# Keys, values and queries of four tiles in one step, and attention one step closer to the convolution

## The reference, cut to what matters

```python
t = _to_tokens(x)
t = t + _L1_attn_ref(_ln_t(t), Wq, Wk, Wv)     # causal, one head of 128, softmax over the tokens before
t = t + _L1_ffn_ref(_ln_t(t), gate_w, gate_b, weight1, weight2)
```

## Time and profile before

| what | value |
|---|---|
| median of 3 runs | 2902.15 us (2899.94 to 2903.96) |
| the profiled execution | 2897.93 us, its span 2895.9 us |
| busy share PE, PEld, DVE, ACT, POOL | 93%, 73%, 65%, 62%, 61% |
| mean granted TensorE clock of the span | 0.977 |
| images 1 to 6, each | about 327.6 us |

### The profile page before, as it was taken

How to read it: one execution, slowest core, us unless ns; L and a number is a source line. 1 busy time by engine, 2 the same in 40 slices (tenths; PEclk the granted TensorE clock), 3 DMA queues, 4 the chain that set the end, 5 groups by cost and what they waited for, 6 DMA issues and landing times. The chain is left out here.

```text
span 2895.9 us, 53454 instructions
## 1 busy us (share of the span) xinstructions
PE 2702.8 (93%) x19102; PEld 2123.3 (73%) x19102; DVE 1887.0 (65%) x7235; ACT 1785.9 (62%) x4118; POOL 1758.3 (61%) x1831
## 2 busy tenths in 40 slices
PE   5688999999999999999999999999999998899787
PEld 3466787778777887778777787778777787777664
DVE  3466675767577775866677775866677766765425
ACT  3455666666675666666676666666676666665430
POOL 5777775776577755776577755776577756750000
PEclk8899999999999999999999999999999999999889
DMA  6455334633255324633255323643255323432199
GB/s 187 119 148 139 112 114 120 169 110 103 86 158 140 109 86 118 164 117 98 88 156 141 113 84 118 155 124 97 85 158 152 116 84 95 126 82 95 28 397 394
DMA packets 218212, 382.59 MB, mean 132 GB/s; under 512 B 43849, under 2 KB 128777, under 8 KB 217051
## 3 DMA queue, kind: packets, MB, share of 16 engines
q0 software_dynamic: 88992, 250.76, 30.0%
q1 hardware_dynamic: 126363, 113.95, 13.1%
q10 hardware_dynamic: 2592, 14.45, 1.2%
HBM read 316.90 MB, written 62.13 MB: 131 GB/s over the span
## 5 line engine op out<-in xcount | busy, mean ns | idle before, releaser
L532 POOL DMA_INDIRECT shared<-pair_table,idx x1800 | 1737.8, 965 | 836.4 <-issue 527.7
L1144 PEld LDWEIGHTS bank_o<-vals,prob_t 128*128 128x128 f32 x5200 | 634.4, 192 | 130.3 <-ACT prob_t L579 65.3
L1144 PE MATMUL bank_o<-vals,prob_t 128*128 128x128 f32 x5200 | 663.2, 277 | 31.5 <-ACT prob_t L579 31.5
L579 ACT ACTIVATE prob_t<-bank_r 128x512 f32<-128x512 f32 (+3 forms) x728 | 383.3, 548 | 479.8 <-PE bank_r L1131 479.0
L834 DVE CUSTOM_DVE_ANT_0 prob<-bank_r,mask 128x512 f32<-128x512 f32 (+3 forms) x728 | 449.9, 628 | 310.4 <-PE bank_r L1122 308.0
L1122 PE MATMUL bank_r<-keys,qt 128*128 128x512 f32 (+3 forms) x1456 | 640.7, 556 | 0.0
L824 DVE SCALAR_TENSOR_TENSOR shared<-shared,wb 128x128 f32<-128x128 f32 x1800 | 516.6, 347 | 160.4 <-ACT shared L560 159.7
L560 ACT ACTIVATE shared<-shared,wa 128x128 f32<-128x128 f32 x1800 | 561.6, 392 | 42.7 <-DMA shared<-pair_table,idx 42.6
L1111 PEld LDWEIGHTS bank_r<-convw_t,smp_t 128*128 128x128 f32 x3600 | 444.2, 194 | 56.8 <-issue 36.3
L1111 PE MATMUL bank_r<-convw_t,smp_t 128*128 128x128 f32 x3600 | 477.5, 279 | 1.5 <-ACT smp_t L565 1.5
L1131 PE MATMUL bank_r<-ident,prob 128*128 128x128 f32 x2600 | 382.2, 274 | 13.8 <-ACT prob L657 13.8
(11 more groups left out here) (168 smaller groups left out, 2235.7 us busy)
## 6 DMA issues: line engine op xcount, KB each, us to landing
shared<-in_dram SPq DMA_DIRECT2D x32, 1024.0 KB, 17.9
shared<-pair_table,idx POOLq DMA_INDIRECT x1800
pair_table<-rows_out SPq DMA_DIRECT2D x112, 256.0 KB
t<-in_dram SPq DMA_DIRECT2D x48, 256.0 KB, 3.9
t_dram<-t SPq DMA_DIRECT2D x48, 256.0 KB
shared<-in_dram SPq DMA_DIRECT2D x7, 1568.0 KB
stage<-t_dram POOLq DMA_DIRECT2D x8, 832.0 KB, 7.5
pm_dram<-logit SPq DMA_DIRECT2D x8, 800.0 KB
```

Of the source, the lines that this page charges most:

```text
L532: pool.indirect_dma_start(g[t % RING][:, n, :], None, pair_table[b % 2], bass.IndirectOffsetOnAxis(ap=idx[:, b % 2, i * TAPS + n:i * TAPS ...
L579: act.activation(prob_t[q % 3][:, 0:w], ring_bank(("prob", t, c))[:, 0:w], ACT.Copy)\
L1144: last = pe.matmul(attn_ps, prob_t[q % 3][:, n * P:(n + 1) * P], vals[:, slot(tb, at), :], start=(at == 0), stop=(at == ti))
```

## The change

It sets the three lags to 5, 6 and 7 and moves "keys", "vals" and "query" of each group into the one step 4n + 4: keys at F, vals at M, query at L. Before, keys were at L of that step and vals and query in the step after. All other units keep their places.

```diff
-LAG_S, LAG_V, LAG_T = 6, 7, 8
+LAG_S, LAG_V, LAG_T = 5, 6, 7
 MISC = (
-    (0, "E", "vals", -1, 5), (0, "M", "query", -1, 5), (0, "L", "keys", -1, 6),
-    (1, "E", "vals", -1, 6), (1, "M", "query", -1, 6),
+    (0, "F", "keys", -1, 6), (0, "M", "vals", -1, 6), (0, "L", "query", -1, 6),
     (2, "L", "turn_xf", -1, 4),
     (3, "E", "logit", -1, 4), (3, "F", "gstat", 1, 0),
-    (4, "L", "keys", 0, 0),
-    (5, "E", "vals", 0, 0), (5, "M", "chunk", 1, 0), (5, "L", "query", 0, 0),
+    (4, "F", "keys", 0, 0), (4, "M", "vals", 0, 0), (4, "L", "query", 0, 0),
+    (5, "M", "chunk", 1, 0),
     (6, "M", "chunk", 1, 1), (6, "L", "turn_xf", -1, 5),
     (7, "E", "logit", -1, 5), (7, "F", "turn", 1, 0), (7, "M", "chunk", 1, 2), (7, "L", "turn_xf", -1, 6),
-    (8, "E", "logit", -1, 6), (8, "M", "chunk", 1, 3), (8, "L", "keys", 0, 1),
-    (9, "E", "vals", 0, 1), (9, "F", "turn", 1, 1), (9, "M", "chunk", 1, 4), (9, "L", "query", 0, 1),
+    (8, "E", "logit", -1, 6), (8, "F", "keys", 0, 1), (8, "M", "chunk", 1, 3), (8, "M", "vals", 0, 1), (8, "L", "query", 0, 1),
+    (9, "F", "turn", 1, 1), (9, "M", "chunk", 1, 4),
     (10, "M", "chunk", 1, 5),
     (11, "F", "turn", 1, 2), (11, "M", "chunk", 1, 6),
-    (12, "F", "turn", 1, 3), (12, "M", "pm", -1, 0), (12, "L", "keys", 0, 2), (12, "L", "pm", -1, 1),
-    (13, "E", "vals", 0, 2), (13, "F", "pm", -1, 2), (13, "M", "query", 0, 2), (13, "L", "pm", -1, 3),
+    (12, "F", "turn", 1, 3), (12, "F", "keys", 0, 2), (12, "M", "pm", -1, 0), (12, "M", "vals", 0, 2), (12, "L", "pm", -1, 1), (12, "L", "query", 0, 2),
+    (13, "F", "pm", -1, 2), (13, "L", "pm", -1, 3),
     (14, "M", "pooled", -1, 0), (14, "L", "turn_xf", 0, 0), (14, "L", "turn_pooled", -1, 0),
     (15, "E", "logit", 0, 0), (15, "L", "turn_xf", 0, 1),
-    (16, "E", "logit", 0, 1), (16, "L", "keys", 0, 3),
-    (17, "E", "vals", 0, 3), (17, "M", "query", 0, 3),
+    (16, "E", "logit", 0, 1), (16, "F", "keys", 0, 3), (16, "M", "vals", 0, 3), (16, "L", "query", 0, 3),
...
```

## The result

| | before | after |
|---|---|---|
| median | 2902.3 us (2899.9 to 2904.0, 4 runs) | 3062.6 us (3059.3 to 3067.3, 4 runs) |
| ratio, 95% interval | | 1.056 (1.0546 to 1.0573) |
| span of the profiled execution | 2895.9 us | 3062.1 us |
| mean granted clock of the span | 0.977 | 0.965 |
| images 1 to 6, each | 325.9 to 327.6 us | 348.4 to 351.7 us |

The change makes the kernel 160 us slower; 3068 us was forecast. In kernel.py of after every line from the table on stands three lines higher: L1029 is L1032 of before, L1059 is L1062, L1100 is L1103.

The account below looks back on a forecast made before the run. PE's own queue was taken as the bound, except early in image 0, where POOL sets the pace. Terms 108 + 38.5 + 30 - 5 - 5 = 166.5 us on 2897.9 us gave 3064 us, stated as a 3068 us median; range 2985 to 3135 us.

Parts of the forecast that it names:

- Term 1: Keys steps of each image: at F, PE waits for DVE's normalising, 1.4 to 3.5 us each; 108 us in all.
- Term 2: Step 14, images 1 to 7: DVE's gate rows wait for "pooled" of the same step, PE loses 5.5 us; 38.5 us.
- Term 3: PE's clock: 2.5 more stretches per image at the lower level behind the new holes, 1.7 us each; 30 us.
- Terms 4 and 5: Pipeline drained one step earlier, -5 us; shifted waits for samples (steps 16, 17) and exponential (step 6 to 5), -5 us.
- Rival A: PE's existing idle time swallows the holes, later waits vanish, clock stays up: 78 us slower, 2980 us; 13%.
- Rival B: Each new hole on PE brings the lower clock: 95 us instead of 30, 3133 us; 8%.
- Rival C: Not slower: PE, 73% full by weight loads, has room for the stalls; only term 4's gain is left, 2893 us; 6%.

Follow-up runs that it names:

- the table without the lags: Kernel before with the new places of keys, vals and query but old lags 6, 7, 8: 3031.7 us, 1.046; on a slow chip 3804.3 us, 0.979.
- the third run of the gate's rows: Changed kernel with only the gate's normalised rows written at the old lag of 8: 3015.6 us, 1.040 to the kernel before.
- both repairs: Changed kernel with keys at M, query at L, vals at E of the next step, gate's rows one step later: 2879.3 us, 0.993; slow chip 3921.4 us, 1.008.

## Why the prediction was right, and where its terms were off

The time (3068 us forecast, 3062.6 us measured) and the direction came from two waits that the kernel before does not have, and each was found where it had been put. The span grew by 166.2 us. By the two traces that is 100.4 us of waits for keys (103.0 - 2.6), 36.2 us ahead of turn_pooled (36.6 - 0.4), 46.5 us more busy time of PE, and 16.9 us less of all other idle time.

- **Term 1, keys at F: 108 us forecast, 103.0 us measured.** The method held: the end of L897 minus the place that PE would have reached, from one trace, gave 3.45 us for step 4 (3.16 measured), 12.2 + 1.9 us per image (12.3 measured). In step 4 half of the difference is that PE's records overlap: the start of L1131, taken as the place that PE reaches, lies 0.16 us ahead of the recorded end of the taps. The other half is that DVE's rows end earlier, 8.17 us into the step and not 8.35. The table alone, with the old lags, shows 105.9 us of this wait. In image 0 the steps 4, 8 and 12 were costed at nothing. PE did wait there (11.0 us in that image, with 16, 20 and 24), but its idle time did not grow: the image's 6.1 us go with the work that moved there.
- **Term 2, the wait on "pooled": 38.5 us forecast, 36.6 us measured,** 5.15 us against 5.5 us in image 4. The chain on DVE (root, rows, sum, samples, scaling) came out as added up, 6.6 us against 6.7. Writing the gate's rows one step later removes wait and hole.
- **Term 3, the clock: 30 us forecast, some 37 us measured** of the 46.5 us by which PE's busy time grew. This term was too small: in image 4 the lower level holds for 17.1 us instead of 3.4 us, 13.7 us more, where two and a half more stretches of 3.4 us, 8.5 us, were taken. It is four stretches now, one of them twice as long. Three begin within a hole or at most 1.2 us behind one (steps 4, 12 and 14), one behind the older wait for the exponential. The other 9 us of busy time stand in no term. An estimate: ahead of a hole the overlap of two records, 0.16 us, is lost, and some 60 new holes make 10 us. That the hole of step 14 lowers the clock behind it is shown by filling it. For the waits of 1.4 to 3.2 us it is only seen beside them. In the table without the lags the same waits came with 17.1 us of lower level in image 4 and with 3.4 us in image 1, which is 5.5 us shorter (342.9 us).
- **Terms 4 and 5, what is won: -10 us forecast, about -17 us measured,** as what is left over. The idle time ahead of the turning of samples fell by 21.5 us (80.6 to 59.1), half of it in image 0. What the lags bring apart from "pooled" is the third run of the gate's rows against the table without lags: 1.040 against 1.046, 16 to 17 us.

The profiled execution of after takes 3064.1 us, and 3064 us was forecast for it. That this is so near is partly luck. The waits were put too high (146.5 against 136.6 us), PE's busy time too low (30 against 46.5 us), and what is won too low as well (10 against 17 us); these errors cancel.

Rival A (the stalls are swallowed by idle time that PE has) needed 64 us; the older idle time gave up some 17, 12 of them in image 0, where alone it paid for the new waits. Rival B (each hole brings the lower clock) needed 95 us; it was some 37. Rival C was a PE with room, which the weight loads' 73% would allow by the Trainium skill (Perfetto Trace Analysis, Identifying the Most-Contended Engine). Here the gaps in PE's rows decided: a PE that is busy for 318.4 of 327.6 us in an image had no room, and of the 17.5 us of new waits 16.3 us came through as idle time. PE's weight loads are busy for 70% after and 73% before, as the span grew by more than they did.

## What to carry to other kernels

Before a unit is moved ahead in an in-order queue, take from the trace of before when its input is ready and when the queue would get there; the difference, times the number of places, was right here within 5% for the waits. The change cost more than its waits, by the clock behind them. A lag that is made shorter also moves work behind waits that were harmless one step later, so each wait between the parts has to be read again with the new step numbers. With the keys at the first place at which their input is ready, and the gate's rows left at their old lag, the shorter lags beat both kernels: 2879 us against 2899 us and 3063 us.

## What the runs showed of the hardware that was not expected

A hole on TensorE can cost more than its length: 5.15 us idle were followed by a step of 13.03 us at 0.79 of the granted clock, against 10.38 us at 1.00 with the hole filled by 40 turnings. Putting work of no use into the hole made the kernel 16 us faster.

The chips that ran this program differ by a third. On two of them the kernel before takes 3890 us and 3905 us; in all other comparisons it takes 2899 to 2902 us. The waits of PE's weight loads and matmuls for "issue" (for nothing that the profile shows) in the table without the lags, on one of the two:

```profile
PEld bank_o L1141 <- issue: 366.5, 436, 5.6
PE bank_o L1141 <- issue: 239.8, 177, 5.3
```

The row of the same kernel on the other kind of chip:

```profile
PEld bank_o L1141 <- issue: 51.0, 215, 0.3
```

The matmuls have no such wait there. On the first chip they stand still for up to 5.3 us inside runs of products while they wait for no other engine, and the mean clock of that execution is 0.916 instead of 0.970. The order of the kernels is turned round: the table without lags is 2% faster than the kernel before, and both repairs 1% slower. What PE waits for is not in these records. That its instructions come late would fit, and was not tried; the instruction queue moved 2.51 MB in both executions.
